# A graph network of four layers: four row buffers instead of two in the last gather loop

## The chip, the cores and the metric

The kernel runs on one core of a Trainium2 chip. The metric is the device time of one launch in microseconds; the median of several runs counts. The engines are TensorE (PE; its weight loads are listed as PEld), VectorE (DVE), ScalarE (ACT), GpSimd (POOL) and SyncE (SP). GpSimd issues the gathers, SyncE the other loads.

## What is computed

3,125 nodes have 16 features each, and 100,000 edges (`src`, `dst`) join them, sorted by `dst`. Four layers follow one another, each `x = x + layer(relu(layernorm(x)))`. The last phase of the kernel (l3) is the last layer:

```python
def _L3_gnn_ref(features, src, dst):
    ...
    x = features * (out_deg ** (-0.5))[:, None]
    agg = jnp.zeros_like(features).at[dst].add(x[src])
    return agg * (in_deg ** (-0.5))[:, None]
```

The others are an edge-conditioned convolution (phase l0), a tensor-product message layer (l1) and two relational convolutions (l2a, l2b), with the same pattern: fetch a row per edge by one end, make a message, add it up by the other end. Everything is float32.

## The kernel before

**Tiling.** The edges lie in 800 tiles of 125; eight tiles are a chunk, so each of the five phases runs over 100 chunks. Adding up by node is done on TensorE: for each tile a one-hot matrix of the node's high number (392 columns) is the moving operand, and `stationary`, the message in three bf16 parts times a mask of the low number, is the weights. 24 products a chunk go into the PSUM bank `acc` (`add_chunk`, line 665).

**Where the rows come from.** Of the eight tiles of a chunk of l3, four are "far": GpSimd gathers their rows from the table in memory by `indirect_dma_start` (line 649), one instruction for each tile, with the row numbers from `row_numbers`. The other four are "near": TensorE picks blocks of 25 nodes by one-hot products from parts of the table in SBUF (`near_rows`, line 838, 24 products a chunk), VectorE halves the block four times with predicated copies (`near_finish`, line 1424) until one row is left, and ScalarE copies that into `gathered2` beside the far ones (`near_place`, line 1086). `far(ph, s)` is the number of far tiles, `NEAR_OF` the table of near ones.

**Buffers and signals.** `gathered2` has two slots, used by chunk number modulo 2 (`s`). The counter `S[ph]["rows_in"][s]` goes up by 16 with each gather that has landed in a slot. VectorE marks its steps of each chunk in the counter `step`; for l3 they are `is_lo`, `hi`, `rest`, `mid`, `low`, and `low` (line 1321) is the last that reads `gathered2`. GpSimd waits for `low` of the chunk two before, and for its row numbers. SyncE does for each chunk, in this order: wait until the rows of the chunk two before have landed and load the row numbers (line 453, `load_numbers`, two slots); wait for ScalarE's distances and for `low` of the chunk two before and load `fields` (line 500); load the near keys for two chunks on (line 477).

**Order on the engines in l3.** VectorE, for chunk c: two one-hots; wait for the gathered rows of c and for the near rows placed by ScalarE; split the rows in three parts (lines 1312 to 1321) with two more one-hots between; three products that make `stationary` (line 1330); `is_lo` of c+1 (line 1283); `near_finish` of c+2 with the near one-hots of c+3 between its halvings (line 1403). TensorE, for chunk c: wait for `stationary` of c, 24 products into `acc`, then `near_rows` of c+3. So the near rows of c+2 are picked at the end of TensorE's chunk c-1, and VectorE can't begin `near_finish` of c+2 before.

**Loops.** `near_chunks` (line 366) unrolls two chunks, runs a loop of two chunks a pass (`Fori(1, PAIRS - 2)`, 47 passes in l3) and unrolls the last four. GpSimd has `all_chunks` with 49 passes. Each engine runs its own copy of the loop; registers hold the pass number, from which the waits' values are computed.

## Time and profile before

| | us |
|---|---|
| median of three timed runs | 4458.6 (4457.42 to 4461.81) |
| the profiled execution | 4503.67 |
| its span, from the first to the last instruction | 4501.9 |

The profiled execution is slower than the timed ones by 45 us, 1%; its rows give durations and order within its own span. Share of the span in which an engine was busy: PE 96%, PEld 72%, DVE 91%, ACT 72%, POOL 73%. The mean granted TensorE clock was 0.989 of 2.4 GHz. A matmul counts as busy from the start of its reading to its modelled end, so neighbours overlap. In the list of waits, "X <- Y" is the idle time of X before the named group, ended by Y; "issue" means that the profile shows nothing that it waited for, and "remote" a releaser that the profile can't name.

### The profile page before, as it was taken

The numbers are of one execution on the slowest core, as the hardware profiler recorded it, in microseconds if no ns is written. First come the engines' busy times: TensorE is split into PE (matmuls) and PEld (weight loads), VectorE is DVE, ScalarE is ACT, GpSimd is POOL, SyncE is SP. The second block draws the span as 40 slices with busy tenths as digits, with TensorE's granted clock in tenths as the row PEclk, the third lists the DMA queues.
The fourth block names the chain that finished last, engine by engine and source line by source line (L and its number), as shares of the span: only waits on it lengthen the run. The fifth ranks groups of instructions, "written<-read, shape, count | busy, mean of one in ns | idle before, by whom it ended". The sixth has DMA issues, their size and how long they took to land.

```text
span 4501.9 us, 107823 instructions
## 1 busy us (share of the span) xinstructions
PE 4343.3 (96%) x30591; PEld 3227.3 (72%) x30591; DVE 4111.1 (91%) x11847; ACT 3228.1 (72%) x5358; POOL 3306.9 (73%) x2516
## 2 busy tenths in 40 slices
PE   7999999999998999999999999999999998899998
PEld 4767777777775677777767777776777776666666
DVE  7999999999997999999979999997999998888888
ACT  5777777777774777777757777776777776677776
POOL 6788888888884788888847676775676775777776
PEclk8999999999999999999999999999999999999999
DMA  2111111111112322222211111111111111111111
GB/s 59 27 17 18 18 18 17 18 17 18 17 18 55 80 63 63 62 63 62 62 40 27 26 28 27 27 25 42 26 28 27 27 27 25 28 30 30 30 31 25
DMA packets 339795, 152.11 MB, mean 34 GB/s; under 512 B 250726, under 2 KB 325394, under 8 KB 339754
## 3 DMA queue, kind: packets, MB, share of 16 engines
q0 software_dynamic: 104000, 59.31, 10.3%
q1 hardware_dynamic: 235754, 92.30, 8.1%
q8 instruction: 20, 0.33, 0.0%
q14 instruction: 21, 0.17, 0.0%
HBM read 138.66 MB, written 10.00 MB: 33 GB/s over the span
## 4 chain that ended last, share of the span: by engine, by line
PE 66%; DVE 19%; issue 10%; DMA 1%; ACT 1%; DVEq 1%; POOL 1%; another core or an unknown queue 0%; SPq 0%; POOLq 0%; ACTq 0%
PE acc L665 30%; PE rows_ps L838 12%; PE rows_ps L760 7%; PE bank L760 6%; DVE stationary L1330 4%; PE bank L853 3%; DVE one_hot L1302 3%; DVE rows_ps L1424 3%; PE eaT_ps L845 2%; PE rows_ps L748 2%; DVE fields_all L1543 2%; PE rows_ps L669 1%; PE eaT_ps L736 1%; DVE raw L1354 1%; DVE fields_all L1545 1%
## 5 line engine op out<-in xcount | busy, mean ns | idle before, releaser
L665 PE MATMUL acc<-one_hot,stationary 125*128 125x392 bf16 x12000 | 2337.0, 329 | 57.8 <-DVE stationary L1330 33.3
L649 POOL DMA_INDIRECT gathered<-table_l,row_numbers x1200 | 1605.2, 1338 | 452.8 <-issue 333.4
L665 PEld LDWEIGHTS acc<-one_hot,stationary 125*128 125x128 bf16 x12000 | 1147.3, 99 | 734.1 <-DVE stationary L1330 49.9
L956 ACT ACTIVATE distances<-count_hi,fields 125x392 bf16<-125x392 f16 (+1 forms) x2500 | 1222.4, 557 | 0.0
L1330 DVE TENSOR_TENSOR stationary<-mask,parts 125x1024 bf16<-125x1024 bf16 x1500 | 943.6, 683 | 0.2 <-issue 0.2
L941 ACT CAST mask<-is_lo 125x1024 bf16<-125x1024 f32 x500 | 521.7, 1043 | 488.8 <-issue 292.0
L649 POOL DMA_INDIRECT fields_all<-table_l,row_numbers x500 | 673.8, 1348 | 217.6 <-issue 143.2
L1302 DVE TENSOR_SCALAR one_hot<-count_hi,fields 125x392 bf16<-125x392 f16 x2300 | 751.3, 348 | 13.6 <-issue 13.5
L1424 DVE COPY_PREDICATED rows_ps<-near_bits_now,rows_ps 125x320 f32<-125x320 int8 (+3 forms) x1600 | 581.9, 364 | 191.6 <-PE rows_ps L838 121.3
L649 POOL DMA_INDIRECT gathered<-table_l2a,row_numbers x400 | 511.1, 1278 | 265.4 <-DVE parts L1312 122.8
L649 POOL DMA_INDIRECT gathered<-table_l2b,row_numbers x400 | 510.8, 1277 | 244.2 <-DVE parts L1312 121.4
L838 PEld LDWEIGHTS rows_ps<-node_parts,h1T 125*125 125x125 bf16 x7200 | 654.8, 137 | 36.0 <-DVE node_parts L1385 5.7
L969 ACT ACTIVATE one_hot<-distances,ones 125x1568 bf16<-125x1568 bf16 (+1 forms) x400 | 674.0, 1685 | 6.6
L838 PE MATMUL rows_ps<-node_parts,h1T 125*125 125x192 bf16 (+1 forms) x7200 | 672.0, 250 | 5.7 <-DVE node_parts L1385 3.8
L1073 ACT COPY h1T<-eaT_ps 128x500 f32<-128x500 f32 (+1 forms) x300 | 162.1, 540 | 332.9 <-PE eaT_ps L845 314.2
L760 PE MATMUL rows_ps<-w,h1T 128*125 128x256 f32 x1600 | 386.9, 385 | 11.0 <-DVE product L1347 9.2
L1354 DVE TENSOR_REDUCE raw<-product 125x32 f32<-125x512 f32 x400 | 395.1, 1008 | 0.0
L760 PE MATMUL bank<-w,h1T 128*125 128x256 f32 x1600 | 379.8, 380 | 0.0
L760 PEld LDWEIGHTS rows_ps<-w,h1T 128*125 128x125 f32 x1600 | 294.1, 190 | 62.9 <-DVE product L1347 12.8
L760 PEld LDWEIGHTS bank<-w,h1T 128*125 128x125 f32 x1600 | 302.1, 189 | 45.9
L1028 ACT ACTIVATE h1T<-rows_ps,b 128x500 f32<-128x500 f32 x400 | 248.9, 673 | 90.6 <-PE rows_ps L748 84.0
L1403 DVE TENSOR_SCALAR h1T<-near_key,node_key 125x500 bf16<-125x500 f16 (+1 forms) x800 | 307.1, 385 | 2.1 <-DMA near_key<-near_keys_by_chunk 2.0
(221 smaller groups left out, 4807.5 us busy)
## 6 DMA issues: line engine op xcount, KB each, us to landing
near_key<-near_keys_by_chunk SPq DMA_DIRECT2D x300, 122.1 KB
gathered<-table_l,row_numbers POOLq DMA_INDIRECT x1200
fields<-edge_fields SPq DMA_DIRECT2D x500, 31.2 KB
near_key<-near_keys_by_chunk SPq DMA_DIRECT2D x100, 91.6 KB
fields_all<-table_l,row_numbers POOLq DMA_INDIRECT x500
gathered<-table_l2a,row_numbers POOLq DMA_INDIRECT x400
gathered<-table_l2b,row_numbers POOLq DMA_INDIRECT x400
ea<-in_edge_attr SPq DMA_DIRECT2D x100, 62.5 KB
```

The lines of the kernel that those rows point to most:

```text
L649: pool.indirect_dma_start(out=gathered[ph][:, s, t, :], in_=table[ph], out_offset=None, in_offset=bass.IndirectOffsetOnAxis(ap=row_numbers ...
L665: mm = pe.matmul(acc[:, :], stationary[:, s, k, t, :, :].rearrange("p a b -> p (a b)"), one_hot[:, s, t, :], start=first and t == 0 and k ...
L760: mm = pe.matmul(bank[2 + q % 2][0:EP, j * HID:(j + 1) * HID], h1T[:, half, t * EP:(t + 1) * EP], w2[:, half, :], start=half == 0, stop=ha ...
L838: mm = pe.matmul(into.rearrange("p a f -> p (a f)"), near_one_hot[s][:, g, t * EP:(t + 1) * EP], parts_of[:, k, first * f:end * f], start= ...
L941: act.copy(mask[:, s].rearrange("p t a f -> p (t a) f"), is_lo[:, s].rearrange("p t a -> p (t a)")[:, :, None].to_broadcast([EP, T * LO, F ...
L956: ins = act.activation(distances[:, i * n:(i + 1) * n], count_hi[:, 0:n], ACT.Abs, scale=-1.0, bias=fields[:, s, k, t:t + 1].bitcast(F32))
L969: act.activation(into, distances[:, 0:into.shape[1]], ACT.Relu, scale=-1.0, bias=ones[0:EP, 0:1]).then_inc(scalar_hot, 1)
L1302: dve.tensor_scalar(one_hot[:, s, t, :], count_hi[:, :], scalar_field(s, hi_field[ph], t), None, ALU.is_equal)
L1330: ins = dve.tensor_tensor(stationary[:, s, k], mask[:, s], source[:, s, :, k * F:(k + 1) * F][:, :, None, :].to_broadcast([EP, T, LO, F]), ...
L1354: dve.tensor_reduce(raw[:, s, 2 * q:2 * q + 2, :], product[:, q % 2].rearrange("p t i o -> p t o i"), AX.X, ALU.add).then_inc(products_sum ...
L1403: ins = dve.tensor_scalar(near_one_hot[s][:, g, 0:n], near_key[:, s, 0:n], node_key[:, g:g + 1], None, ALU.is_equal)
L1424: return dve.copy_predicated(into, chosen, source)
```

## The change

`gathered2` has four slots instead of two. In l3 the slot of a chunk is its number modulo 4; everything else that has two slots keeps modulo 2. A `Slot` is an integer with the value modulo 2 that also carries `four`, the number modulo 4, and `quad`, the pass. GpSimd waits in l3 for `low` of the chunk four before. The counters of landed rows become four, shared by l2a, l2b and l3, and `rows_in_by` computes the value to wait for, from the rows of the phases before in slots 0 and 1 plus those of this phase. The loops of all five engines in l3 take four chunks a pass (`fours`): 4 chunks unrolled, 23 passes, 4 unrolled; on GpSimd 4 unrolled and 24 passes. The numbers of near tiles are as before.

```diff
--- before.py
+++ after.py
@@ -20,6 +20,7 @@
...
 CHUNKS = TILES // T
 PAIRS = CHUNKS // 2
+QUADS = CHUNKS // 4
@@ -51,6 +52,18 @@
 SRC_KEY, SRC_HI, SRC_LO, DST_HI, DST_LO, DST_WIDE_HI, DST_KEY, TYPE, FIELDS = range(9)
 EPS = 1e-5
+class Slot(int):
+    def __new__(cls, four, quad):
+        self = int.__new__(cls, four % 2)
+        self.four, self.quad = four, quad
+        return self
+    def two_ago(self):
+        return Slot((self.four + 2) % 4, self.quad if self.four >= 2 else self.quad - 1)
 def build(nc, A, out):
@@ -179,7 +192,7 @@
...
-        rows2 = sb("gathered2", [ROWS, 2, T, F])
+        rows2 = sb("gathered2", [ROWS, 4, T, F])
@@ -247,11 +260,26 @@
         PHASES = ("l0", "l1", "l2a", "l2b", "l3")
         S = {}
+        FOUR_SLOTS = ("l3",)
+        AFTER_L1 = ("l2a", "l2b", "l3")
+        rows_in_four = [sem(f"rows_in{q}") for q in range(4)]
         for ph in PHASES:
             S[ph] = {
-                "rows_in": [sem(f"{ph}_rows_in{s}") for s in range(2)],
+                "rows_in": rows_in_four if ph in AFTER_L1 else [sem(f"{ph}_rows_in{s}") for s in range(2)],
                 "step": sem(f"{ph}_vector_step"),
             }
+        def rows_slot(ph, s):
+            return s.four if ph in FOUR_SLOTS else s
+        def rows_in_by(ph, pair, s):
+            if ph not in AFTER_L1:
+                return 16 * far(ph, s) * (pair + 1)
+            of_two = 16 * PAIRS * sum(far(k, s) for k in AFTER_L1[:AFTER_L1.index(ph)] if k not in FOUR_SLOTS)
+            if ph not in FOUR_SLOTS:
+                return of_two + 16 * far(ph, s) * (pair + 1)
+            return (of_two if s.four < 2 else 0) + 16 * far(ph, s) * (s.quad + 1)
         fields_in = [sem(f"fields_in{s}") for s in range(2)]
         numbers_in = [sem(f"row_numbers_in{s}") for s in range(2)]
@@ -347,6 +375,16 @@
             return not isinstance(chunk, int) or chunk >= n
+        def fours(eng, body, first, end, tail):
+            for chunk in range(4 * first):
+                body(chunk, chunk // 2, Slot(chunk % 4, chunk // 4))
+            with eng.Fori(first, end) as quad:
+                for j in range(4):
+                    body(4 * quad + j, 2 * quad + j // 2, Slot(j, quad))
+            for chunk in range(CHUNKS - tail, CHUNKS):
+                body(chunk, chunk // 2, Slot(chunk % 4, chunk // 4))
         def all_chunks(eng, body):
             for s in range(2):
@@ -365,8 +403,11 @@
             for s in range(2):
                 body(CHUNKS - 2 + s, PAIRS - 1, s, s == 1)
-        def near_chunks(eng, body, first=2):
-
+        def near_chunks(eng, body, ph="l1", first=2):
+            if ph in FOUR_SLOTS:
+                fours(eng, body, 1, QUADS - 1, 4)
+                return
             for chunk in range(first):
                 body(chunk, chunk // 2, chunk % 2)
             with eng.Fori(first // 2, PAIRS - 2) as pair:
@@ -445,7 +486,10 @@
                 if later(chunk, 2):
-                    sp.wait_ge(S[ph]["rows_in"][s], 16 * far(ph, s) * pair)
+                    if ph in FOUR_SLOTS:
+                        sp.wait_ge(S[ph]["rows_in"][s.two_ago().four], rows_in_by(ph, pair, s.two_ago()))
+                    else:
+                        sp.wait_ge(S[ph]["rows_in"][s], rows_in_by(ph, pair - 1, s))
                 if ph in rows_d:
                     rows = rows_d[ph][:, bass.ds(chunk, 1), :]
                 else:
@@ -531,7 +575,7 @@
                             sp.wait_ge(table_in, table_in_by("l1"))
                         sp.dma_start(repeated_room[chunk - 2],
                                      turned_d[:, chunk - 2:chunk - 1, :].to_broadcast([LO, F, HI])).then_inc(ev("turned_rows_in"), 16)
-                near_chunks(sp, body, 2 + F if ph == "l1" else 2)
+                near_chunks(sp, body, ph, 2 + F if ph == "l1" else 2)
             def stream_l0():
                 ph = "l0"
@@ -640,17 +684,21 @@
                 def body(chunk, pair, s):
                     pool.wait_ge(numbers_in[s], fields_in_by(ph, pair))
-                    if later(chunk, 2):
-
-                        pool.wait_ge(S[ph]["step"], done(ph, ROWS_READ[ph], chunk - 2))
+                    ahead = 4 if ph in FOUR_SLOTS else 2
+                    if later(chunk, ahead):
+                        pool.wait_ge(S[ph]["step"], done(ph, ROWS_READ[ph], chunk - ahead))
                     pool.sem_inc(ev("chunks_begun"), 1)
                     for t in range(far(ph, s)):
                         pool.indirect_dma_start(
-                            out=gathered[ph][:, s, t, :], in_=table[ph], out_offset=None,
+                            out=gathered[ph][:, rows_slot(ph, s), t, :], in_=table[ph], out_offset=None,
                             in_offset=bass.IndirectOffsetOnAxis(ap=row_numbers[:, s, t:t + 1], axis=0),
-                        ).then_inc(S[ph]["rows_in"][s], 16)
-                all_chunks(pool, body)
+                        ).then_inc(S[ph]["rows_in"][rows_slot(ph, s)], 16)
+                if ph in FOUR_SLOTS:
+                    fours(pool, body, 1, QUADS, 0)
+                else:
+                    all_chunks(pool, body)
             for ph in PHASES:
                 gathers(ph)
@@ -892,7 +940,7 @@
                         near_rows(ph, chunk + 3, 1 - s)
                     if ph != "l3" and follows(chunk, 2):
                         near_messages(ph, chunk + 2, s)
-                near_chunks(pe, body)
+                near_chunks(pe, body, ph)
@@ -1080,10 +1128,11 @@
                 bits = near_bits[:, bass.ds(chunk, 1), keys_of(ph, s)].rearrange("p c k -> p (c k)")
                 act.copy(near_bits_now[:, s, 0:NEAR_OF[ph][s]].bitcast(I8), bits.bitcast(I8)).then_inc(near_bits_in, 1)
-            def near_place(chunk, s):
-
+            def near_place(chunk, four):
+                s = four % 2
                 act.wait_ge(near_picked, chunks_before("l3") + chunk + 1)
-                act.copy(gathered2[:, s, far("l3", s):T, :], near_rows_ps["l3"][s][:, 0:NEAR_OF["l3"][s], 0, :]).then_inc(ev("l3_near_placed"), 1)
+                act.copy(gathered2[:, four, far("l3", s):T, :], near_rows_ps["l3"][s][:, 0:NEAR_OF["l3"][s], 0, :]).then_inc(ev("l3_near_placed"), 1)
             def masks_and_near(ph):
                 def near_result(chunk, s):
@@ -1102,7 +1151,7 @@
                     masks(ph, chunk, s)
                     hi_distances(ph, chunk, pair, s, end=ph == "l2a" or ph == "l2b")
                     if later(chunk, 1) and follows(chunk, 1):
-                        near_result(chunk + 1, 1 - s)
+                        near_result(chunk + 1, (s.four + 1) % 4 if ph == "l3" else 1 - s)
                     if ph == "l1":
                         silus(chunk, s)
@@ -1111,7 +1160,7 @@
                     hi_one_hots(ph, chunk, s, later(chunk, 2))
                     if follows(chunk, 3):
                         near_bits_of(ph, chunk + 3, 1 - s)
-                near_chunks(act, body)
+                near_chunks(act, body, ph)
             def preload(column, function):
@@ -1476,7 +1525,7 @@
                         begin_chunk(ph, chunk + 1, pair + s, 1 - s)
                     if follows(chunk, 2):
                         near_finish(ph, chunk + 2, pair + 1, s, follows(chunk, 3))
-                near_chunks(dve, body)
+                near_chunks(dve, body, ph)
             dve.wait_ge(added, before("l0") + CHUNKS)
@@ -1624,7 +1673,7 @@
                     dve.wait_ge(near_done, chunks_before(ph) + chunk + 1)
                     dve.tensor_tensor(msg[:, s, n:T, :], bank[MESSAGE_BANK[s]][0:EP, 0:(T - n) * F].rearrange("p (t f) -> p t f", f=F),
                                       edge_norm[:, bass.ds(chunk * T + n, T - n)][:, :, None].to_broadcast([EP, T - n, F]), ALU.mult)
-                    dve.wait_ge(S[ph]["rows_in"][s], 16 * n * (pair + 1))
+                    dve.wait_ge(S[ph]["rows_in"][s], rows_in_by(ph, pair, s))
                     st.mark(dve.tensor_tensor(msg[:, s, 0:n, :], gathered2[:, s, 0:n, :],
                                               edge_norm[:, bass.ds(chunk * T, n)][:, :, None].to_broadcast([EP, n, F]), ALU.mult))
                     hot(1)
@@ -1666,9 +1715,9 @@
                 if not later(chunk, 1):
                     one_hots("l3", s, range(T))
                 hot(0, 1)
-                dve.wait_ge(S["l3"]["rows_in"][s], 16 * far("l3", s) * (pair + 1))
+                dve.wait_ge(S["l3"]["rows_in"][s.four], rows_in_by("l3", pair, s))
                 dve.wait_ge(ev("l3_near_placed"), chunk + 1)
-                split(st, gathered2[:, s], lambda k: hot(*((2, 3), (4, 5), (6, 7), ())[k]))
+                split(st, gathered2[:, s.four], lambda k: hot(*((2, 3), (4, 5), (6, 7), ())[k]))
                 to_stationary("l3", chunk, s, parts, lambda: st.wait("low"))
             with_near("l3", l3)
```

GpSimd in l3, before: its loop has two chunks, and each waits for its row numbers and for a step of l3. (`gathered` is `gathered2`, `table_l` the table in memory.)

```order
L354 UNCONDITIONAL_BRANCH
L354 ISA
L645 ISA [waits row_numbers_in0]
L649 DMA gathered<-table_l,row_numbers 125x16 [waits l3_vector_step]
L649 DMA gathered<-table_l,row_numbers 125x16 x3
L645 ISA [waits row_numbers_in1]
L649 DMA gathered<-table_l,row_numbers 125x16 [waits l3_vector_step]
L649 DMA gathered<-table_l,row_numbers 125x16 x3
L354 REGISTER_ALU
L354 COMPARE_AND_BRANCH
```

And now, the unrolled chunks 2 and 3 and the start of the loop:

```order
L694 DMA gathered<-table_l,row_numbers 125x16 [waits row_numbers_in0]
L694 DMA gathered<-table_l,row_numbers 125x16 x3
L694 DMA gathered<-table_l,row_numbers 125x16 [waits row_numbers_in1]
L694 DMA gathered<-table_l,row_numbers 125x16 x3
L382 UNCONDITIONAL_BRANCH
L382 ISA
L690 ISA [waits row_numbers_in0]
L694 DMA gathered<-table_l,row_numbers 125x16 [waits l3_vector_step]
```

Chunks 2 and 3 no longer wait for a step of VectorE; from chunk 4 on they do, and every chunk waits for its row numbers as before.

VectorE at the end of the loop's second chunk, before (L1424 is the last halving, L1302 the one-hots of the next chunk, behind the loop):

```order
L1444 REGISTER_ALU
L1424 COPY_PREDICATED rows_ps<-near_bits_now,rows_ps 125x4x16 [waits near_rows_halved]
L372 REGISTER_ALU
L372 COMPARE_AND_BRANCH
L1302 TENSOR_SCALAR one_hot<-count_hi,fields 125x392 [waits chunk_added]
```

The same place now:

```order
L1493 REGISTER_ALU
L1473 COPY_PREDICATED rows_ps<-near_bits_now,rows_ps 125x4x16 [waits near_rows_halved]
L1351 TENSOR_SCALAR one_hot<-count_hi,fields 125x392 [waits chunk_added]
L1351 TENSOR_SCALAR one_hot<-count_hi,fields 125x392
L1719 REGISTER_ALU [waits rows_in2]
L1361 CAST parts<-gathered 125x8x16 [waits l3_near_placed]
```

The branch is gone from this place and comes after the fourth chunk; the third chunk waits for rows in slot 2.

## Rows read from the trace of the kernel before

**Rows 1.** Busy time by stretch: the loops of l0 and l3, first branch to last

```profile
core 0: us, PE busy (x) PEld busy (x) DVE busy (x) ACT busy (x) POOL busy (x), PEclk, DMA share, GB/s
88.90:1349.70 1260.80, 1246.36 (x7149) 909.57 (x7148) 1208.90 (x2633) 940.40 (x1687) 1023.82 (x751) 1.00 0.14 19
...
3864.70:4473.00 608.30, 569.25 (x4419) 408.87 (x4418) 535.44 (x1659) 457.78 (x737) 470.11 (x369) 1.00 0.19 30
```

**Rows 2.** The same view of four chunks in a row, from TensorE's first product of each

```profile
4046.02:4052.75 6.73, 6.20 (x50) 4.42 (x49) 5.88 (x18) 4.83 (x8) 5.51 (x5) 1.00 0.19 23
4052.75:4060.00 7.25, 6.22 (x49) 4.44 (x49) 5.67 (x20) 5.02 (x8) 5.08 (x5) 1.00 0.17 29
4060.00:4066.38 6.38, 6.21 (x48) 4.43 (x49) 5.87 (x19) 4.91 (x8) 5.06 (x5) 1.00 0.18 30
4066.38:4072.43 6.05, 6.05 (x48) 4.46 (x49) 5.54 (x19) 5.09 (x9) 4.83 (x5) 1.00 0.21 37
```

**Rows 3.** Who waited for whom in the last loop: us in total, times, longest

```profile
POOL gathered L649 <- DVE parts L1321: 30.5, 23, 2.3
...
PE acc L665 <- DVE stationary L1330: 28.6, 34, 2.1
DVE rows_ps L1424 <- PE rows_ps L838: 28.2, 44, 1.6
...
DVE one_hot L1302 <- issue: 13.2, 45, 0.3
DVE rows_ps L1424 <- remote: 10.5, 7, 2.2
```

**Rows 4.** Order of time, VectorE: start, duration, what, [idle before it, releaser]

```profile
4046.36 0.50 DVE L1424 COPY_PREDICATED rows_ps<-near_bits_now,rows_ps 125x320 f32<-125x320 int8 x1 [0.64 <-PE rows_ps L838]
...
4048.57 0.55 DVE L1302 TENSOR_SCALAR one_hot<-count_hi,fields 125x392 bf16<-125x392 f16 x2 [0.29 <-issue]
4049.04 0.22 DVE L1312 CAST parts<-gathered 125x128 bf16<-125x128 f32 x1
4049.18 0.89 DVE L1302 TENSOR_SCALAR one_hot<-count_hi,fields 125x392 bf16<-125x392 f16 x2
...
4050.81 1.89 DVE L1330 TENSOR_TENSOR stationary<-mask,parts 125x1024 bf16<-125x1024 bf16 x3
...
4054.20 0.50 DVE L1424 COPY_PREDICATED rows_ps<-near_bits_now,rows_ps 125x320 f32<-125x320 int8 x1 [1.36 <-remote]
...
4057.84 0.29 DVE L1321 TENSOR_TENSOR parts<-rest,parts 125x128 bf16<-125x128 f32 x1
4058.05 1.89 DVE L1330 TENSOR_TENSOR stationary<-mask,parts 125x1024 bf16<-125x1024 bf16 x3
```

**Rows 5.** The same, GpSimd's gathers

```profile
4048.79 1.21 POOL L649 DMA_INDIRECT gathered<-table_l,row_numbers  x1 [0.30 <-issue]
...
4059.03 1.39 POOL L649 DMA_INDIRECT gathered<-table_l,row_numbers  x1 [1.25 <-DVE parts L1321]
```

**Rows 6.** The same, SyncE's loads

```profile
4058.36 0.26 SPq L500 DMA_DIRECT2D fields<-edge_fields  x1
...
4059.66 0.26 SPq L453 DMA_DIRECT2D row_numbers<-in_src  x1
```

**Rows 7.** Last phase, groups (busy us, mean ns), then one line's shortest, median, longest ns

```profile
L649 POOL DMA_INDIRECT gathered<-table_l,row_numbers x385 | 492.9, 1280 | 145.6 <-issue 100.4 <-DVE parts L1321 33.1 <-DVE is_lo L1283 7.6
...
L1302 DVE TENSOR_SCALAR one_hot<-count_hi,fields 125x392 bf16<-125x392 f16 x392 | 129.3, 371 | 13.5 <-issue 13.5
...
L1302 DVE TENSOR_SCALAR one_hot<-count_hi,fields x392: 302/316/736, 3850.1 to 4489.2; 125x392 bf16<-125x392 f16 x196
```

**Rows 8.** DMA queues in the last loop, all that have packets there

```profile
q1 hardware_dynamic: 35880, 14.82, 9.6%
q0 software_dynamic: 11747, 3.36, 9.2%
```

**Rows 9.** The chain that ended last, in order of time

```profile
4485.92 2.89 DMA gathered<-table_l,row_numbers
```

## The prediction

> **What bounds the kernel now.** I read the stretches first, then the last loop chunk by chunk, then who waits there, then single instructions. In the loops of l0 to l2b TensorE is nearly always busy (in l0's 1246.36 of 1260.80 us), but in the last phase's loop it is busy for 569.25 of 608.30 us [rows 1]. The change touches only this loop and the chunks unrolled around it. 47 branches lie in that stretch, so 46 passes of two chunks take 608.3 / 92 = 6.61 us a chunk. Four chunks in a row took 6.73, 7.25, 6.38 and 6.05 us, 26.41 together [rows 2], and the whole loop repeats about this pattern. The shortest, 6.05, is TensorE without a pause. The 6.38 differs from it by the loop's branch alone, 0.33 us. The other two are chunks in which TensorE waited for VectorE's `stationary` (28.6 us in 34 waits) [rows 3].
>
> So VectorE's chain is late in half of the chunks. It is also tied to TensorE: it waits for the near rows that TensorE picks (28.2 us in 44 waits, plus 10.5 us in 7 waits whose releaser the profile does not name) [rows 3]. From halving those near rows at 4046.36 to the end of `stationary` at 50.81 + 1.89 = 4052.70 the chain took 6.34 us; from 4054.20 to 4059.94 it took 5.74 us [rows 4]. TensorE needs 6.05 for its part, and the chain must fit inside that and the handover. In the first chain two things stick out: 0.29 us at the branch, and a pair of one-hots that took 0.89 instead of 0.55 us, +0.34 [rows 4]. The second of them ended at 4050.07, just behind the end of GpSimd's gather of 4048.79 (1.21 us long) [rows 5].
>
> What the gathered rows themselves cost: VectorE has no wait for them in the loop's list of waits; GpSimd waits for VectorE to have read the old rows (`low`, L1321) 30.5 us in 23 waits [rows 3], a wait of an engine on which nobody waits.
>
> **The change part by part.** (a) Four row buffers. GpSimd may start a chunk's gathers when the chunk four before is read, not two before. The 30.5 us of waits fall away, and nothing on the path gets earlier by that, for VectorE does not wait for the rows. What comes next as GpSimd's limit is the row numbers, which still have two buffers: SyncE loads them behind the loads of `fields`, and that load still waits for `low` of two chunks back. After `low` of 4057.84 + 0.29 = 4058.13 [rows 4], SyncE issued fields at 58.36, near keys at 58.88 and the next chunk's numbers at 59.66 [rows 6]. So numbers leave at best 1.5 us after `low` of three chunks before and then have to arrive; the nearest transfer with a duration is a gather, 2.89 us [rows 9]. That makes a start 4.4 us after that `low`, where today's gather starts 0.9 us after the next one (4059.03) [rows 5], that is 6.6 + 0.9 = 7.5 us after it. The lead gained is some 3 us, half a chunk: the fourth buffer is hardly used.
>
> (b) GpSimd's own rate. A gather takes 1280 ns on average [rows 7] and 0.30 us pass between two [rows 5]: 4 x 1.58 = 6.3 us a chunk. Undisturbed it is 4 x 1.51 = 6.05. If the rest of the loop went at 6.1 us, GpSimd would be the next limit at about 6.3. The first gather of a chunk now runs beside `stationary` and is stretched, 1.39 us at 4059.03 [rows 4, 5].
>
> (c) Collisions with GpSimd. In the last phase VectorE's one-hots average 371 ns where their median is 316 [rows 7]. 392 x 0.055 = 22 us, some 0.22 us a chunk. With freed gathers these meetings move. Bounds: all gone, -0.22 us a chunk; or one more of 0.34 us in each chunk. A meeting matters only in a chunk where VectorE is the late one, about half of them now. I take -0.05 us a chunk, which is nearer to no change (halved for the chunks that count, the bounds are -0.11 and +0.17), with a lean to less, since the gathers are no longer started by `low` at the same point of each chain: 96 x -0.05 = -5 us. This is the least certain term.
>
> The Trainium skill (SBUF — State Buffer, Who interferes with whom) says that casts and tensor_scalar operations in a two-port mode and GpSimd exclude each other through a shared port, the first to start holding it for its whole instruction. The trace agrees that one blocks the other (0.89 us above), but not for the whole instruction: the cast at 4049.04 took its 0.22 us inside the gather of 4048.79 [rows 4, 5]. By the page nearly every such operation would be held up, before as after; this term would be nothing and the sum -7 us.
>
> (d) Loops of four chunks on all five engines. The branch is passed 24 times less on each. On TensorE it costs 0.33 us (6.38 - 6.05) [rows 2], on VectorE 0.29 us (13.2 us in 45 waits) [rows 3]. In each group of four, one branch lies in a chunk bound by TensorE and one in a chunk bound by VectorE's chain, and the engines pass them side by side. Whichever goes, 24 x 0.31 = -7 us. If the delayed chain also no longer makes VectorE see the near rows late (1.36 us at 4054.20) [rows 4], more goes: that is a rival below.
>
> (e) At nothing: the three waits that are now on shared counters have constants in place of others and the same number of instructions in l2a and l2b; the larger buffer is memory only; GpSimd's loop now starts two chunks later and needs no tail. Register work per chunk is the same by the order of instructions, hidden by VectorE's and TensorE's data work. If that cover failed, it would be one register instruction, under 0.1 us, in 24 passes: 2 us.
>
> Sum: -7 - 5 = -12 us. The profiled execution took 4503.67 us (span 4501.9), the three timed runs 4458.6 in the median, 1% less. The span's loop is part of both; 12 us scaled by 0.99 is still 12: 4458.6 - 12 = 4446.6, say 4447.
>
> **The rivals.** *Only the branches (no gain from the buffers).* GpSimd was off the path and stays there; meetings with VectorE change places but not their number. For it: no VectorE wait for rows [rows 3]. Against: four chunks lock to GpSimd's start at `low`, and a lock of another phase need not cost the same. It gives -7 to -3 us, 4452 to 4456.
>
> *Worse meetings (slower).* Freed, a chunk's gathers would start some 3.5 to 4.4 us after a `low` instead of 0.9, one every 1.51 us, and so lie otherwise over the near-key one-hots, the two pairs of one-hots and the casts. Where a gather's later half meets one of these, it costs up to the 0.34 us above. One more block of 0.34 us in each chunk, effective in two of three chunks, is 96 x 0.23 = +22 us, less 7: 4474. It decides once the added blocks exceed 0.07 us a chunk on the path. For it: the kernel has a chain of 5.74 us undisturbed against 6.05, so little slack. Against: in the chunks of 6.05 and 6.38 us VectorE is ahead and absorbs a block.
>
> *The cascade ends (much faster).* If VectorE fits into TensorE's time in every chunk, a group of four takes 4 x 6.05 + 0.33 = 24.53 us instead of 26.41: 24 x 1.88 = -45 us, 4414. GpSimd's 6.3 us a chunk speaks against it; by that limit it is 96 x (6.61 - 6.3) = -30 us, 4429.
>
> *The loop is too long for the instruction store (slower).* The longest pass on TensorE has been l0's (48 passes, 7149 / 48 = 149 products and as many weight loads [rows 1]); the last loop's had 4419 / 46 = 96 and now has 192, each with a weight load. No instruction packets are in the last loop now, only the two data queues [rows 8]. If each pass had to fetch again, it would be one stall per block. The trace shows no such stall; it is bounded by nothing below and, above, by the longest pause of the pattern that no engine explains, 1.36 us [rows 4]; with two a pass 24 x 2.7 = +65 us, less 12: 4512. The Trainium skill (Runtime: NRT & Kernel Launch, Instruction fetch mechanics) says that a branch whose target is outside a window of two pages of 16 KiB stalls on a fetch, which speaks against this change; the same section gives TensorE a larger store, by which nothing would happen. No loop of the kernel before is long enough to tell.
>
> *The change doesn't do what it says* is in part my expectation: with two buffers of row numbers the gathers get about one chunk ahead, not two.
>
> **How the numbers follow.** Chances: the forecast 0.40 (4434 to 4450), only the branches 0.25 (4450 to 4458), worse meetings 0.20 (4460 to 4485), the cascade ends 0.10 (4412 to 4432), instruction store 0.05. 0.2% is 8.9 us, about what a measurement of this kernel can tell from no change. Faster: nearly all of the forecast's case and all of the cascade's, less a little, 0.46. Same: the branches' case, the upper edge of the forecast's and the lower of the slower one's, 0.32. Slower: 0.22. The range goes from 4424 to 4478: it takes in the 30 us of GpSimd's limit, most of the slower case, and leaves out the far ends.
>
> **What would show it.** In the last loop's stretch: time per chunk 6.61 before; 6.48 by the forecast, 6.54 by the branches alone, 6.14 if the cascade ends, above 6.7 if meetings get worse. GpSimd's waits for `low` should vanish and be replaced by waits for row numbers; VectorE's waits at the branch should be 24 instead of 46; the one-hots' mean of 371 ns tells whether meetings got fewer. Instruction packets inside the loop would show the last rival. The prediction is wrong if the loops of l0 to l2b change, or if VectorE waits for gathered rows.

## The result

The changed kernel took 4467.75 us in the median (4459.38 to 4474.51), the kernel before, timed beside it, 4459.64 us: a ratio of 1.0015, with an interval of 1.0009 to 1.0021. That is 8 us slower, within the 0.2% that I had called no change, but on the other side from the -12 us of the forecast. Timed again on two occasions, the same kernel came to 1.0030 (1.0018 to 1.0042) and 1.0020 (1.0011 to 1.0029).

Its profiled execution took 4470.26 us (span 4468.3), near its own median. That of the kernel before, on which the prediction rests, took 4503.67 us. Laid side by side the two profiles show a gain of 33 us where the timing shows a loss of 8. So the first experiment was another profile of the kernel before; it comes below, and the comparison with it is the one that counts.

The profile of the changed kernel, the chain that ended last, by engine and by line:

```profile
PE 75%; DVE 11%; issue 5%; DMA 5%; ACT 2%; POOL 2%; DVEq 0%; SPq 0%; POOLq 0%; ACTq 0%
PE acc L713 34%; PE rows_ps L886 13%; PE rows_ps L808 8%; PE bank L808 5%; PE bank L901 4%; DMA gathered<-table_l,row_numbers 3%; PE eaT_ps L893 2%; PE rows_ps L720 2%; DVE stationary L1379 2%; PE rows_ps L796 2%; DVE raw L1403 2%; DVE one_
```

The landing of gathered rows, 3% of the span, is now a link of the chain (in the page of the kernel before, all DMA has 1%). The stretches that answer to [rows 1] and [rows 2], l0's loop, the last loop, and four chunks of it in a row (columns as there):

```profile
88.00:1349.00 1261.00, 1250.67 (x7187) 913.86 (x7187) 1214.21 (x2646) 945.52 (x1697) 1022.93 (x755) 1.00 0.14 19
3869.40:4437.10 567.70, 544.46 (x4227) 390.38 (x4226) 520.29 (x1586) 434.36 (x705) 460.95 (x351) 1.00 0.20 31
...
4114.10:4120.71 6.61, 6.21 (x48) 4.43 (x49) 5.99 (x20) 4.91 (x8) 5.40 (x4) 1.00 0.22 31
4120.71:4127.29 6.58, 6.21 (x48) 4.44 (x49) 6.07 (x20) 4.91 (x8) 5.36 (x4) 1.00 0.19 29
4127.29:4133.91 6.62, 6.21 (x48) 4.43 (x49) 5.99 (x20) 4.91 (x8) 5.40 (x4) 1.00 0.17 28
4133.91:4140.49 6.58, 6.21 (x48) 4.43 (x49) 5.80 (x20) 4.91 (x8) 5.36 (x4) 1.00 0.20 32
```

l0's loop is what it was. In the last one the four chunks shown take the same 6.6 us each. That holds for about half of the loop: counted from TensorE's first product of a chunk to that of the next, 41 of 88 chunks take 6.57 to 6.69 us, 10 still take the bare 6.05 of TensorE, and the others 6.09 to 7.17. Two first products at the loop's start, 6.05 us apart:

```profile
3871.38 4.15 PE L713 MATMUL acc<-one_hot,stationary 125*128 125x392 bf16 x24 [0.36 <-DVE stationary L1379]
...
3877.43 4.14 PE L713 MATMUL acc<-one_hot,stationary 125*128 125x392 bf16 x24
```

22 passes of four chunks fill 567.7 us, 6.45 us a chunk. The waits in that stretch, which answer to [rows 3]:

```profile
PE acc L713 <- DVE stationary L1379: 22.9, 57, 1.0
DVE parts L1361 <- DMA gathered<-table_l,row_numbers: 14.6, 35, 0.6
POOL gathered L694 <- DMA row_numbers<-in_src: 11.0, 36, 0.3
...
DVE one_hot L1351 <- issue: 6.2, 21, 0.3
DVE rows_ps L1473 <- PE rows_ps L886: 6.0, 16, 0.6
```

VectorE waits for gathered rows 35 times; in [rows 3] it never did. Its waits for TensorE's near rows fell from 44 to 16, and its branch waits from 45 to 21. The groups that answer to [rows 7]:

```profile
L694 POOL DMA_INDIRECT gathered<-table_l,row_numbers x372 | 489.1, 1315 | 114.1 <-issue 89.0 <-DMA row_numbers<-in_src 11.0 <-DVE is_lo L1332 7.3
L1351 DVE TENSOR_SCALAR one_hot<-count_hi,fields 125x392 bf16<-125x392 f16 x376 | 118.4, 356 | 6.5 <-issue 6.5
```

The one-hots became shorter (371 to 356 ns) and the gathers longer (1280 to 1315 ns). The second number holds the answer. The first does not: in `e1_base`, the kernel before profiled again, the one-hots take 357 ns between 3900 and 4400 us, against 353 there in the changed kernel. GpSimd and VectorE in order of time, within the four chunks above (start, duration, what, idle before):

```profile
4114.22 1.21 POOL L694 DMA_INDIRECT gathered<-table_l,row_numbers  x1 [0.30 <-DVE is_lo L1332]
4115.73 1.21 POOL L694 DMA_INDIRECT gathered<-table_l,row_numbers  x1 [0.30 <-issue]
4117.25 1.25 POOL L694 DMA_INDIRECT gathered<-table_l,row_numbers  x1 [0.30 <-issue]
4118.80 1.73 POOL L694 DMA_INDIRECT gathered<-table_l,row_numbers  x1 [0.30 <-DMA row_numbers<-in_src]
4120.84 1.21 POOL L694 DMA_INDIRECT gathered<-table_l,row_numbers  x1 [0.30 <-DVE is_lo L1332]
...
4123.86 1.21 POOL L694 DMA_INDIRECT gathered<-table_l,row_numbers  x1 [0.30 <-issue]
4125.38 1.73 POOL L694 DMA_INDIRECT gathered<-table_l,row_numbers  x1 [0.30 <-DVE parts L1367]
```

```profile
4118.77 1.89 DVE L1379 TENSOR_TENSOR stationary<-mask,parts 125x1024 bf16<-125x1024 bf16 x3
...
4123.00 0.84 DVE L1351 TENSOR_SCALAR one_hot<-count_hi,fields 125x392 bf16<-125x392 f16 x2 [0.29 <-issue]
4123.77 0.21 DVE L1361 CAST parts<-gathered 125x128 bf16<-125x128 f32 x1
...
4124.68 0.42 DVE L1367 CAST parts<-rest 125x128 bf16<-125x128 f32 x1
...
4125.34 0.69 DVE L1379 TENSOR_TENSOR stationary<-mask,parts 125x1024 bf16<-125x1024 bf16 x1
```

GpSimd has 0.30 us between two gathers, whatever releaser is named: nothing holds it. Gathers start 1.51 us apart (1.55 behind the one of 1.25 us), except the one that starts just behind VectorE's first product (4118.80 behind 4118.77): it takes 1.73 us instead of 1.21, and the next start is 2.04 us on. Four starts take 3 x 1.51 + 2.04 = 6.57 us, the length of the chunk. The last gather of a chunk (4120.84) lands 2.54 us later, at 4123.38. In three of the four chunks VectorE waits for such a landing; in this one, which holds its branch, it casts the rows at 4123.77 without a wait. 1.57 us after that its products start, again on top of a gather, and in this pattern each chunk pays the 0.53 us once.

The two meet there because the step before ties them together. VectorE's cast of 4124.68 falls into the gather of 4123.86 and takes 0.42 us, where it takes 0.21 when it meets none. It ends at 4125.10, just behind that gather (4125.07). The first product then starts 0.24 us after the cast's end and the next gather 0.30 us after the gather's end, so that the gather comes 0.03 to 0.04 us behind the product. Between 3900 and 4400 us the 18 traces of this case have 672 gathers of 1.73 to 1.75 us, and each of them starts at that distance and follows such a held cast.

### The profile page after: what moved, and what is told of

Read it like the earlier page. It is cut to its first block, busy times and chain, and to the rows that moved or that the text cites. A ratio compares the mean times of both kernels' runs of the same rounds, so it can differ in the third digit from the quotient of the medians.

```text
span 4468.3 us, 107407 instructions
## 1 busy us (share of the span) xinstructions
PE 4337.5 (97%) x30591; PEld 3245.1 (73%) x30591; DVE 4131.2 (92%) x11847; ACT 3225.3 (72%) x5358; POOL 3313.0 (74%) x2516
## 4 chain that ended last, share of the span: by engine, by line
PE 75%; DVE 11%; issue 5%; DMA 5%; ACT 2%; POOL 2%; DVEq 0%; SPq 0%; POOLq 0%; ACTq 0%
PE acc L713 34%; PE rows_ps L886 13%; PE rows_ps L808 8%; PE bank L808 5%; PE bank L901 4%; DMA gathered<-table_l,row_numbers 3%; PE eaT_ps L893 2%; PE rows_ps L720 2%; DVE stationary L1379 2%; PE rows_ps L796 2%; DVE raw L1403 2%; DVE one_hot L1351 1%; POOL gathered L694 1%; DVE rows_ps L1473 1%; PE eaT_ps L784 1%
## 5 line engine op out<-in xcount | busy, mean ns | idle before, releaser
L694 POOL DMA_INDIRECT gathered<-table_l,row_numbers x1200 | 1608.9, 1341 | 427.5 <-issue 326.7
L694 POOL DMA_INDIRECT gathered<-table_l2b,row_numbers x400 | 512.5, 1281 | 237.0 <-DVE parts L1361 114.9
L1452 DVE TENSOR_SCALAR h1T<-near_key,node_key 125x500 bf16<-125x500 f16 (+1 forms) x800 | 324.9, 407 | 2.9 <-DMA near_key<-near_keys_by_chunk 2.8
```

What stands on the lines that cost most here:

```text
L694: pool.indirect_dma_start(out=gathered[ph][:, rows_slot(ph, s), t, :], in_=table[ph], out_offset=None, in_offset=bass.IndirectOffsetOnAxis ...
L1452: ins = dve.tensor_scalar(near_one_hot[s][:, g, 0:n], near_key[:, s, 0:n], node_key[:, g:g + 1], None, ALU.is_equal)
```

## Experiments

### The kernel before, profiled again; and which part of the change costs

`e1_base` is the kernel before, `e1_again` the changed one. The two others change one line of it, the first new line in `e1_ahead2`, the second in `e1_ahead3`:

```diff
-                    ahead = 4 if ph in FOUR_SLOTS else 2
+                    ahead = 2
+                    ahead = 3 if ph in FOUR_SLOTS else 2
```

> The kernel before, unchanged, profiled on the same chip as the next three. The profiled execution of before that the prediction rests on took 4503.7 us, 44 us above the median of its timed runs; that of the changed kernel lies within 3 us of its own. If the last loop has more than one pattern, and that execution fell in a slow one, the loop shows here about 6.3 to 6.4 us per chunk instead of 6.61 and the span is 4455 to 4465 us. If the profile only stretches everything, the loop shows 6.6 again and the profiled execution is again about 4500 us.

> The changed kernel, unchanged, on the same chip. The ratio to before should be 1.001 to 1.002 again (+5 to +9 us). In its last loop 6.45 us per chunk, VectorE waiting for gathered rows some 35 times for 0.4 us each.

> The changed kernel, with its loops of four chunks and its four row slots, but GpSimd waits for the low half of the rows of the chunk two before, as in the kernel before: only the loops of four are left of the change. Theory A (the freed gathers cost what was measured, the loops of four bring their 7 us): ratio 0.998 to 0.999, 4450 to 4455 us, no VectorE waits for gathered rows. Theory B (the loops of four cost it, for instance by a fixed pattern of four chunks): 1.001 to 1.002, as the changed kernel. Theory C (neither: branches bring nothing, and the freed gathers cost 8 us): 1.000.

> The changed kernel, with GpSimd held by the low half of the chunk three before instead of four. Row numbers have two buffers, so a lead of three chunks is already more than GpSimd can reach: theories A and C give the time of the changed kernel, 1.001 to 1.002, and so does B. Another time than that would say that the wait for the chunk four before is sometimes the one that holds GpSimd.

Measured: 4460.7 us (0.9999, 0.9990 to 1.0007), 4473.3 (1.0030, 1.0018 to 1.0042), 4473.9 (1.0031, 1.0021 to 1.0041) and 4474.5 (1.0036, 1.0023 to 1.0049). So holding GpSimd as before gains nothing: theory A fell and B stood. All three changed kernels came out above the 1.001 to 1.002 that was expected of them; their intervals overlap, so `e1_ahead3` shows no difference from `e1_again`. The freed gathers are not the cost; something in the loops of four is.

The profiled execution of `e1_base` took 4463.4 us, like its timed runs, and its last loop is not the one of [rows 2]. Four chunks in a row:

```profile
4000.22:4006.27 6.05, 6.05 (x48) 4.46 (x49) 5.54 (x19) 5.09 (x9) 4.83 (x5) 1.00 0.21 39
4006.27:4013.02 6.75, 6.21 (x52) 4.43 (x49) 5.90 (x19) 4.83 (x8) 5.53 (x5) 1.00 0.19 24
4013.02:4019.07 6.05, 6.05 (x49) 4.46 (x50) 5.53 (x19) 5.11 (x9) 4.83 (x5) 1.00 0.19 38
4019.07:4025.80 6.73, 6.21 (x51) 4.43 (x49) 5.88 (x19) 4.82 (x8) 5.51 (x5) 1.00 0.19 24
```

Its waits between 3900 and 4400 us, then GpSimd's gathers as a group there, then some of them in order of time:

```profile
DVE rows_ps L1424 <- PE rows_ps L838: 25.2, 39, 0.7
PE acc L665 <- DVE stationary L1330: 20.5, 39, 0.5
```

```profile
L649 POOL DMA_INDIRECT gathered<-table_l,row_numbers x313 | 404.6, 1293 | 95.4 <-issue 81.7 <-DVE is_lo L1283 11.9 <-DMA row_numbers<-in_src 1.8
```

```profile
4050.43 1.36 POOL L649 DMA_INDIRECT gathered<-table_l,row_numbers  x1 [0.30 <-issue]
4052.09 1.21 POOL L649 DMA_INDIRECT gathered<-table_l,row_numbers  x1 [0.30 <-issue]
4053.61 1.21 POOL L649 DMA_INDIRECT gathered<-table_l,row_numbers  x1 [0.30 <-issue]
4055.12 1.74 POOL L649 DMA_INDIRECT gathered<-table_l,row_numbers  x1 [0.30 <-issue]
4057.16 1.21 POOL L649 DMA_INDIRECT gathered<-table_l,row_numbers  x1 [0.30 <-DVE is_lo L1283]
```

Two chunks take 6.05 + 6.74 = 12.79 us, 6.39 a chunk, all through the loop. VectorE waits for near rows once in two chunks and for gathered rows never. GpSimd is without a pause here too: the waits for `low` of [rows 3], up to 2.3 us long, are gone. Its eight gathers meet the products twice, at 1.36 and at 1.74 us: 8 x 1.51 + 0.15 + 0.53 = 12.76. The execution behind the prediction differs from this one by 40 us of span: 20 us had gone before the last phase began (3834.8 us against 3814.9, at its first one-hot), 20 us within it.

From here on each kernel's last loop is told by one number of the trace: how many gathers GpSimd started between 3900 and 4400 us. With four to a chunk, 2000 us over that count is the time per chunk, good to 0.02 us. Beside it stands how many of them took 1.73 us or more, and the time of the profiled execution, to which these columns belong.

| kernel | median us | ratio | profiled us | gathers in 500 us | mean ns | of them 1.73 us | us per chunk | VectorE's waits for rows |
|---|---|---|---|---|---|---|---|---|
| before, first profile | | | 4503.7 | 304 | 1277 | 18 | 6.58 | 0 |
| e1_base | 4460.7 | 0.9999 | 4463.4 | 313 | 1293 | 39 | 6.39 | 0 |
| changed, first profile | 4467.8 | 1.0015 | 4470.3 | 309 | 1317 | 50 | 6.47 | 34 |
| e1_again | 4473.3 | 1.0030 | 4473.2 | 307 | 1327 | 56 | 6.51 | 40 |
| e4_again | 4466.7 | 1.0020 | 4478.0 | 304 | 1342 | 72 | 6.58 | 53 |
| e1_ahead2 | 4473.9 | 1.0031 | 4463.1 | 309 | 1314 | 48 | 6.47 | 35 |
| e1_ahead3 | 4474.5 | 1.0036 | 4482.0 | 305 | 1338 | 67 | 6.56 | 48 |
| e2_quad_all | 4478.2 | 1.0037 | 4476.0 | 305 | 1341 | 73 | 6.56 | 52 |
| e2_quad_dve | 4480.9 | 1.0043 | 4475.2 | 308 | 1326 | 58 | 6.49 | 48 |
| e2_quad_rest | 4462.5 | 1.0006 | 4459.2 | 313 | 1292 | 39 | 6.39 | 0 |
| e3_three_base | 4453.1 | 0.9990 | 4452.4 | 237 (three a chunk) | 1263 | 0 | 6.33 | 0 |
| e3_three_again | 4442.0 | 0.9961 | 4442.9 | 242 (three a chunk) | 1347 | 24 | 6.20 | 0 |
| e3_late_again | 4453.9 | 0.9987 | 4453.9 | 316 | 1281 | 19 | 6.33 | 0 |
| e4_late_again | 4454.7 | 0.9987 | 4454.7 | 316 | 1281 | 18 | 6.33 | 0 |
| e4_late_quad | 4452.9 | 0.9984 | 4452.5 | 319 | 1268 | 11 | 6.27 | 17 |
| e4_late_base | 4448.1 | 0.9976 | 4448.4 | 320 | 1262 | 0 | 6.25 | 0 |

But for the first row, where GpSimd still waited for `low`, every row with four gathers is 4 x (mean + 0.304) us long, within 0.03: the differences lie in the gathers' mean. For `e1_base` against the changed kernel's first profile this makes 96 x (6.47 - 6.39) = 8 us, the timed loss. One profile stands for one execution, though: the changed kernel's three range over 6.47 to 6.58, the last of them, of e4_again, is 11 us above that kernel's median, and the profile of e1_ahead2 is 11 us below its own. Where the mean goes up, it is by more gathers of 1.73 us: 39 in about 78 chunks of e1_base, 50 to 72 in the changed kernel, 18 and 19 with the edit of the one-hots that comes last.

### Whose branch?

Loops of four chunks in the kernel before, its two slots kept. `near_chunks` gets a second form, and each engine is given it or not:

```diff
+            if by_four:
+                for chunk in range(4):
+                    body(chunk, chunk // 2, chunk % 2)
+                with eng.Fori(1, QUADS - 1) as quad:
+                    for j in range(4):
+                        body(4 * quad + j, 2 * quad + j // 2, j % 2)
...
-                near_chunks(dve, body)
+                near_chunks(dve, body, by_four=ph == "l3")
```

> The kernel before, with its two row slots, and every engine's loop of the last phase over four chunks instead of two. Theory B (the rarer branches let VectorE catch up with GpSimd, whose gathers then set the pace at 6.58 us per chunk where one of them lies under the products): ratio 1.002 to 1.004, VectorE waits for gathered rows in more than half of the chunks. Theory A2 (it is the four slots or their counts that cost it): 0.998 to 1.000 and no such waits.

> The kernel before, with VectorE's loop of the last phase alone over four chunks; TensorE, ScalarE, GpSimd and SyncE keep their loops of two. Theory B, if VectorE's own branch is what matters: 1.002 to 1.004, as with all engines. If it is TensorE's branch: 1.000, with the pattern of 12.79 us per two chunks kept.

> The other half: all engines but VectorE loop over four chunks in the last phase. Theory B with VectorE's branch as the cause: the pattern of 12.79 us per two chunks stays, ratio 0.999 to 1.000. With TensorE's or GpSimd's branch as the cause: 1.002 to 1.004.

Measured 1.0037 (1.0024 to 1.0050), 1.0043 (1.0030 to 1.0056) and 1.0006 (0.9998 to 1.0015). VectorE's branch alone makes the difference. With it every two chunks the pattern of 12.79 us stays, whatever the other four engines do; with it every four chunks VectorE meets the landing of the rows 48 to 52 times in 500 us. The waits of `e2_quad_dve`:

```profile
DVE parts L1322 <- DMA gathered<-table_l,row_numbers: 21.1, 48, 0.6
DVE rows_ps L1434 <- PE rows_ps L848: 1.0, 3, 0.6
```

If that is so, 0.3 us of anything on VectorE in the middle of the four chunks should bring the old pattern back:

```diff
+        pad = sb("pad", [EP, 160])
...
+                    if ph == "l3" and s.four == 1:
+                        dve.tensor_tensor(pad[:], pad[:], pad[:], ALU.mult)
```

> The changed kernel with one more VectorE operation (a product of a scratch row of 160 numbers with itself, some 0.3 us, about the time of a branch) at the end of every fourth chunk, two chunks after the branch, so that VectorE loses as much every two chunks as it did in the kernel before. Theory B: the pattern of 12.79 us per two chunks comes back and the time falls to 1.000 (6.40 us per chunk instead of 6.45 to 6.57), although VectorE has 23 operations more. If the time lost were simply VectorE's work, it would rise by 0.3 x 23 = 7 us, to 1.0045.

> The kernel of e2_pad (the changed one with a VectorE operation of 0.3 us in the middle of each four chunks), with GpSimd held by the chunk two before, as in the kernel before. There the pattern of two chunks had come back but at 13.04 us instead of 12.79. If the missing hold made the difference, 12.79 us is here and the ratio is 0.999 to 1.001, and the four buffers' free gathers cost 0.13 us per chunk in that pattern. If the operation itself costs it, 13.04 us and 1.005 or more again.

Measured: 1.0092 (1.0067 to 1.0117) and 1.0103 (1.0074 to 1.0132). The first is against both of its theories; for e3_pad_hold the second one came true, 13.04 us and more than 1.005. In the last loop half of the forecast came true: a fixed pattern of two chunks (7.18 and 5.86 us from `low` to `low`) without waits for rows in `e2_pad` and with 4 in `e3_pad_hold`, but of 13.04 us, not 12.79. The gathers say why, 1325 ns on average. In each two chunks one starts 0.03 us behind the first product (1.73 us), one 0.88 us behind it (1.49), and one 0.75 us ahead (1.33): 0.52 + 0.28 + 0.12 = 0.92 us of stretch instead of 0.68. Whether GpSimd is held by the chunk two or four before made no difference. The rest of the loss has nothing to do with the last phase: e3_pad_hold enters it 35 us later than e1_base, e2_pad 8 us later, most of it lost in l0's loop. The added buffer stands ahead of others and so moves them, but it is the same in both kernels, and the 27 us between them are not explained by it; their timed runs scatter over 40 us and more (4484 to 4525, 4479 to 4523). The cause stays open. The total times of these two prove nothing; only their last loops are used.

### Does GpSimd set the pace?

Three of the four gathers of a chunk, from the third chunk on (for the changed kernel from the fifth), in both kernels. They leave the fourth group of rows out: its place keeps the rows of the first chunks, so what l3 adds up is not the layer's result. The edit of the kernel before (in the changed one the same counts stand in `rows_in_by`):

```diff
-                    sp.wait_ge(S[ph]["rows_in"][s], 16 * far(ph, s) * pair)
+                    sp.wait_ge(S[ph]["rows_in"][s], 16 * far(ph, s) * pair if ph != "l3" else 48 * pair + 16)
...
-                    for t in range(far(ph, s)):
+                    for t in range(3 if ph == "l3" and later(chunk, 2) else far(ph, s)):
...
-                dve.wait_ge(S["l3"]["rows_in"][s], 16 * far("l3", s) * (pair + 1))
+                dve.wait_ge(S["l3"]["rows_in"][s], 48 * (pair + 1) + 16)
```

> The kernel before, but in the last phase each chunk from the third on gathers three of its four far groups of rows and leaves the fourth as the first chunks left it (its output is wrong in l3 for that): GpSimd has 4.5 us of work per chunk instead of 6.0. Theory G (GpSimd's gathers set the pace of the last phase in both kernels): the loop falls from 6.39 to 6.05 to 6.2 us per chunk, 18 to 32 us off, 0.993 to 0.996. Theory V (the chain of VectorE, TensorE and near rows sets it in the kernel before, and GpSimd only keeps up): 6.3 to 6.39 us per chunk, 0.998 to 1.000, less what collisions are gone.

> The changed kernel with the same three of four gathers. Theory G: no VectorE waits for gathered rows, 6.05 to 6.15 us per chunk, 4 to 8 us below the kernel before with three gathers (the branches, at last), so 0.991 to 0.995. Theory V: about 6.3, and still slower than or equal to the other with three gathers.

Measured: 4453.1 us (0.9990, 0.9981 to 1.0000) and 4442.0 us (0.9961, 0.9947 to 0.9976). A quarter of GpSimd's work is worth 7 us in the kernel before, and 25 to 31 us in the changed one (4466.7 or 4473.3 less 4442.0). Both theories were half right: V for the kernel before, whose chain of VectorE, TensorE and near rows takes 6.33 us a chunk in this run, just below GpSimd's 6.39; G for the changed one, whose chain takes 6.20 (expected were 6.05 to 6.15) while GpSimd needs 6.5. Fewer gathers also block VectorE less. In the kernel before its one-hots fell from 357 to 348 ns and the cast of L1318 from 276 to 253 ns, 4 x 0.009 + 0.023 = 0.06 us a chunk, which is all that was gained; so this run does not show that GpSimd alone held that kernel at 6.39. In the changed kernel VectorE has no wait for rows left; its waits in the same stretch:

```profile
DVE rows_ps L1473 <- PE rows_ps L886: 19.5, 44, 0.7
...
PE acc L713 <- DVE stationary L1379: 8.2, 22, 0.6
```

Between the two of them, 11 us: that is what the whole change brings where GpSimd is out of the way. How much of it is the loops of four was not told apart from the slots: with two slots, GpSimd still waits there for VectorE to have read the old rows (140.8 us in 73 waits between 3900 and 4400 us).

### Does the place of the gathers matter?

The same one-hots, later: the products then start 0.47 us later after the rows have landed.

```diff
-                hot(0, 1)
                 dve.wait_ge(S["l3"]["rows_in"][s.four], rows_in_by("l3", pair, s))
                 dve.wait_ge(ev("l3_near_placed"), chunk + 1)
-                split(st, gathered2[:, s.four], lambda k: hot(*((2, 3), (4, 5), (6, 7), ())[k]))
+                split(st, gathered2[:, s.four], lambda k: hot(*((0, 1), (2, 3), (4, 5), (6, 7))[k]))
```

`late_again` is this edit on the changed kernel, `late_quad` on e2_quad_all (loops of four, two slots), `late_base` on the kernel before.

> The changed kernel, with VectorE's first two one-hots of a chunk in the last phase made behind the first cast of the rows instead of ahead of the wait for them: the same work, but the products start 0.47 us later after the rows have landed. If the period of 6.58 us is four gathers at 1.51 plus 0.53 by which the products stretch the third of them, and that stretch hangs on the gather starting just behind the products' start, then the gathers now stand 0.47 us earlier against the products, the stretch falls to 0.15 to 0.3, and the loop takes 6.2 to 6.35 us per chunk: 12 to 25 us below the changed kernel, 0.997 to 0.999. If the place of the gathers does not matter, 1.002 to 1.004 as before, or more since the wait comes earlier.

> The changed kernel once more. 1.0015 to 1.003, in its last loop four gathers of 1.51 us plus some 0.45 to 0.5 us of stretch per chunk: 6.45 to 6.55 us.

> The changed kernel with the later one-hots of e3_late_again once more: 0.998 to 0.9995, stretch of 0.30 us per chunk, 6.33 us.

> The kernel before with loops of four chunks in the last phase (as e2_quad_all: two row slots) and the later one-hots. If the four slots matter to nothing, it takes the time of e4_late_again within 0.1%, 0.998 to 0.9995. If the hold of two slots costs, as e2_quad_all's 1.0037 beside 1.003 for four slots might say, 1.000 to 1.001.

> The kernel before with the later one-hots alone, its loops of two chunks and two slots kept. Its pattern of 12.79 us per two chunks is set by two chains of nearly equal length: 12.65 to 12.7 without the fourth gather, and the gathers with their stretch. So it gains at most the 0.05 us per chunk by which they differ, 4 to 5 us (0.999), if the stretch falls, and nothing, or a loss of up to 10 us (1.002), if the new place of the one-hots brings the gathers under the products more often.

Measured: e3_late_again 4453.9 us (0.9987, 0.9978 to 0.9995), e4_late_again 4454.7 (0.9987, 0.9978 to 0.9996), e4_late_quad 4452.9 (0.9984, 0.9975 to 0.9993), e4_late_base 4448.1 (0.9976, 0.9966 to 0.9986), beside e4_again at 4466.7 (1.0020). An edit that adds and removes no work takes 12 us off the changed kernel (4466.7 to 4454.7 on the same chip), through a stretch of 4 x (1.281 - 1.209) = 0.29 us a chunk instead of 0.53. (The two profiled executions are 23 us apart, since that of e4_again was its slowest; its loop took 6.58 us a chunk, just over the 6.45 to 6.55 expected.) The forecast of 6.2 to 6.35 us a chunk held. In this form two slots do as well as four (4452.9 and 4454.7, intervals that overlap): the four buffers themselves brought nothing that can be measured. With the one-hots in their old place, two slots and loops of four on all engines gave 1.0037 and four slots 1.0015 to 1.0030 in other sessions, so some us may lie between them there.

My expectation for late_base was wrong: I allowed it 5 us, since the other chain took 6.33 us a chunk, and it gained 12. It is the fastest kernel here that makes all four gathers, below even e3_three_base with its three. So the later one-hots shorten VectorE's and TensorE's chain too; by how much each of the two counts there is open. VectorE's last cast of a chunk is never held by a gather in it (0 of 80; in e4_again 72 of 76). Its gathers in two chunks, and VectorE's products among them:

```profile
4051.19 1.21 POOL L649 DMA_INDIRECT gathered<-table_l,row_numbers  x1 [0.30 <-issue]
4052.70 1.21 POOL L649 DMA_INDIRECT gathered<-table_l,row_numbers  x1 [0.30 <-issue]
4054.22 1.21 POOL L649 DMA_INDIRECT gathered<-table_l,row_numbers  x1 [0.30 <-issue]
4055.73 1.22 POOL L649 DMA_INDIRECT gathered<-table_l,row_numbers  x1 [0.30 <-issue]
...
4058.76 1.25 POOL L649 DMA_INDIRECT gathered<-table_l,row_numbers  x1 [0.30 <-issue]
4060.31 1.30 POOL L649 DMA_INDIRECT gathered<-table_l,row_numbers  x1 [0.30 <-issue]
4061.91 1.50 POOL L649 DMA_INDIRECT gathered<-table_l,row_numbers  x1 [0.30 <-issue]
```

```profile
4054.57 1.89 DVE L1330 TENSOR_TENSOR stationary<-mask,parts 125x1024 bf16<-125x1024 bf16 x3
...
4060.44 1.89 DVE L1330 TENSOR_TENSOR stationary<-mask,parts 125x1024 bf16<-125x1024 bf16 x3
```

The first products meet gathers that start 0.35 us ahead of them and 1.16 us behind their start, and neither is stretched. The second meet one 0.13 us ahead (1.30 us) and one 1.47 us behind (1.50). None starts just behind a first product, and the 1.73 us is gone. 8 x 1.51 + 0.45 = 12.53 us for two chunks.

## Why the prediction was wrong

**The ground of the sum.** "46 passes of two chunks take 608.3 / 92 = 6.61 us a chunk" described one execution. The prediction divided out its 1% and went on; but the 1% was not spread over it. Half of it lay in the last loop, as a pattern of four chunks with late near rows that the typical execution does not have: 6.39 us, and 6.05 us of TensorE in every other chunk. The prediction's "late in half of the chunks" was also not what its row said, 34 waits in 92 chunks; it is true of e1_base, with 39 in 78. A forecast of 6.48 us a chunk was about met (6.45), yet from the true start it was a loss. Had I read the 45 us between profile and timed runs as a warning about the pattern, the gain of 0.13 us a chunk would have had no room to come from.

**(a) Four buffers, no gain.** Right in its sum. The lead is not used, but for another reason than the row numbers' two buffers: GpSimd never gets ahead at all. "VectorE does not wait for the rows" failed: it waits 35 times, which the prediction had named as a sign that it is wrong.

**(b) GpSimd's own rate.** The step that failed. I wrote 6.3 us a chunk and called it the next limit "If the rest of the loop went at 6.1 us". In the kernel before GpSimd already had no pause, at 6.39 us a chunk (e1_base), and the limit itself is no constant: 6.04 us plus a stretch of 0.2 to 0.53 us, set by where the gathers lie against the products. "The first gather of a chunk now runs beside `stationary` and is stretched" had the mechanism in hand and gave it no price.

**(c) Collisions.** Taken at -5 us, from the one-hots' side. The 371 ns belonged to that first, untypical execution; against e1_base the one-hots hardly changed (357 to 353 ns), while two other operations of VectorE met gathers more often. First e1_base, then the changed kernel, between 3900 and 4400 us:

```profile
L1403 DVE TENSOR_SCALAR h1T<-near_key,node_key 125x500 bf16<-125x500 f16 x156 | 53.6, 344 | 0.0
L1318 DVE CAST parts<-rest 125x128 bf16<-125x128 f32 x79 | 21.8, 276 | 2.7
...
L1452 DVE TENSOR_SCALAR h1T<-near_key,node_key 125x500 bf16<-125x500 f16 x154 | 61.1, 397 | 0.0
L1367 DVE CAST parts<-rest 125x128 bf16<-125x128 f32 x77 | 30.3, 393 | 2.7
```

That is 2 x 0.053 + 0.117 = 0.22 us a chunk more on VectorE. On GpSimd it is 4 x (1317 - 1293) ns = +0.10 us a chunk, some 9 us, and the loop goes at GpSimd's pace. So the term had the wrong sign: it was read from one operation of VectorE in an untypical execution, and nothing was priced on the engine without idle time.

**(d) The branches.** -7 us. With three gathers the whole change is worth -11 us, the branches among it; in the changed kernel none of it arrives, since VectorE's branch had kept it out of step with the landing rows (e2_quad_dve, e2_quad_rest). So the chain of VectorE and TensorE would have been 11 us shorter, and the loop became 8 us longer all the same, because the gathers, whose pace it now follows, went from 6.39 to 6.47 us a chunk.

**(e) At nothing**, and the loops of l0 to l2b unchanged: as forecast.

**The rivals.** "Worse meetings" gave 4460 to 4485 us and has the sign and the size. The near-key one-hots and the casts that it named were blocked more, as (c) shows, but that is not what made the loop longer: VectorE waits for rows in 35 chunks. What it did not price is the gather that is stretched. "Only the branches" and "the cascade ends" did not happen; GpSimd's limit, which I had named against the latter, is what forbade them. No instruction fetch stalled the longer loop: the last loop of the changed kernel has one instruction packet in 567.7 us:

```profile
q14 instruction: 1, 0.01, 0.0%
```

The rule on the shared port, that whoever is first holds it for the whole instruction (the Trainium skill, SBUF — State Buffer, Who interferes with whom), speaks of both engines, and I had weighed it for one. By the trace it holds only in part: three products in a row of 1.89 us stretch a gather by 0.53, 0.09 to 0.29 or 0 us, depending on where it starts, and VectorE's cast of 4124.68 was held to the gather's end, while the one of 4123.77 took its 0.21 us though a gather began under it at 4123.86.

What stays open: why VectorE's and TensorE's chain with three gathers takes 6.33 and 6.20 us where TensorE has 6.05 us of work plus a branch; what share of e4_late_base's gain is this chain's; what chooses between the two patterns of the kernel before, of which I saw the slow one once; and what costs the two padded kernels their time before the last phase.

## What to carry to other kernels

Before a profile is taken as the kernel, hold its time against the timed runs: 1% too much can be one loop in another rhythm, and then its slack is not there to be won. Where an engine has no idle time beyond the gap between its instructions, it is at its limit, even if nobody is seen to wait for it; price a collision on that engine, and on every operation that can meet it. Making a loop's other engines faster by a branch can bring them onto the landing of data and fix them there; moving two short operations past the wait was worth 12 us, where the branches and the buffers together cost 6 to 13.

## What the runs showed of the hardware

A gather's 1.21 us on GpSimd depends sharply on its start against a run of three VectorE products (bf16, 0.68 us each, starting 0.60 us apart). Between 3880 and 4400 us of e1_base, e4_again, e4_late_base and e2_pad:

| start against the first product | mean duration, us | end against the first product |
|---|---|---|
| 0.75 us ahead | 1.33 | 0.58 |
| 0.36 us ahead | 1.21 | 0.85 |
| 0.13 us ahead | 1.30 | 1.17 |
| 0.03 us behind | 1.73 | 1.77 |
| 0.88 us behind | 1.49 | 2.37 |
| 1.01 us behind | 1.36 | 2.37 |
| 1.16 us behind | 1.22 | 2.37 |
| 1.47 us behind | 1.50 | 2.97 |

The last column has the order in it. A gather that is stretched ends at one of a few points, 0.60 us apart like the products: of 1480 gathers longer than 1.25 us that start from 1 us ahead of a first product to 1.6 us behind it (all 18 traces, 3900 to 4400 us), 1432 end within 0.03 us of 0.58, 1.17, 1.77, 2.37 or 2.97 us. One whose 1.21 us are over just ahead of such a point is hardly stretched; one that would end just behind a point can go on to the next. Why is not shown, and not every gather follows it (the one 0.36 us ahead is not stretched at all).

0.16 us of start decides over 0.44 us. Each engine moves the other: a gather holds a cast of VectorE to its end, and the products behind the cast stretch the next gather. So a kernel can keep the rhythm that it falls into: e1_base repeated 5.67 and 7.12 us to within 0.02 us through its whole loop, while the changed kernel went in and out of its 6.58.
